# Eight banks and a cap by VectorE in the time-step units, the first dense experts' results copied by ScalarE, and the head's image and text tiles in turns

## What is computed

```python
h = concat([patches @ W_proj.T + b_proj + pos_emb, table[positions(x_txt)]])   # (32, 68, 256)
x = layernorm(h)
u = x @ W_x.T + b_x; g = sigmoid(x @ W_g.T + b_g)                  # 256 -> 512
u = u * g + (conv3(u) + conv_b) * (1 - g)
dt = clip(softplus(x @ W_dt.T + b_dt).mean(axis=(0, 1)), 1e-3, 2)  # mean over all rows
A_d = exp(-softplus(A_raw) * dt); B_d = (A_d - 1) / (A + 1e-6) * B_ssm
y = scan of  state = A_d * state + B_d * u_t,  y_t = sum(state * C_ssm)   # 16 states
h = h + layernorm(x + y @ W_out.T + b_out) * ln_g + ln_b
x = layernorm(h)
top 2 of 4 experts by softmax(layernorm(x) @ router_w.T)
hid = relu(layernorm(x @ w1[e]) * ln_g[e] + ln_b[e])               # 256 -> 512
h = h + layernorm(weighted sum of hid @ w2[e])
```

## Time and profile before

| | us |
|---|---|
| median of 3 runs | 486.98 (486.80 to 487.05) |
| the profiled execution, its own time | 486.0 |
| its span in the trace | 484.2 |
| mean granted clock of PE | 0.979 |

### The profile page before, as it was taken

How to read it: one execution, slowest core, us unless ns; L and a number is a source line. 1 busy time by engine, 2 the same in 40 slices (tenths; PEclk the granted TensorE clock), 3 DMA queues, 4 the chain that set the end, 5 groups by cost and what they waited for, 6 DMA issues and landing times.

```text
span 484.2 us, 10063 instructions
## 1 busy us (share of the span) xinstructions
PE 444.6 (92%) x3208; PEld 375.2 (77%) x3208; DVE 334.0 (69%) x1000; ACT 309.5 (64%) x708; POOL 154.5 (32%) x247
## 2 busy tenths in 40 slices
PE   7988988889899999999998979999999999999982
PEld 5768976767678878878887867878878888888862
DVE  6696645767999334334888968897857548864694
ACT  1773449677965464316666657777787677776882
POOL 5000013484000000002233376377467634526012
PEclk8899999899999999989999989999999999999998
DMA  7944169500029842983511122022222225321421
GB/s 176 198 156 121 48 205 332 175 0 1 1 62 260 201 116 59 219 247 90 196 45 33 67 76 79 11 75 91 84 83 77 78 87 186 104 74 56 142 63 57
DMA packets 54159, 53.62 MB, mean 111 GB/s; under 512 B 24888, under 2 KB 47708, under 8 KB 52828
## 3 DMA queue, kind: packets, MB, share of 16 engines
q1 hardware_dynamic: 50428, 44.46, 34.1%
q0 software_dynamic: 2784, 7.63, 4.2%
q10 hardware_dynamic: 896, 0.89, 0.6%
HBM read 32.40 MB, written 20.58 MB: 109 GB/s over the span
## 4 chain that ended last, share of the span: by engine, by line
PE 48%; DVE 13%; ACT 5%; issue 4%; DMA 4%; SPq 1%; DVEq 0%; ACTq 0%; POOLq 0%
PE bank L1090 12%; PE bank L921 9%; PE bank L461 5%; PE bank L463 4%; PE bank L462 4%; PE bank L997 4%; PE bank L1077 3%; PE bank L941 3%; DVE bsth L1721 1%; PE bank L989 1%; PE bank L1058 1%; ACT U L498 1%; DMA got<-expert_y 1%; DMA xg<-sorted_x 1%; DMA out_dram<-acc 1%
## 5 line engine op out<-in xcount | busy, mean ns | idle before, releaser
L1090 PE MATMUL bank<-w,hr 128*128 (+1 forms) x384 | 92.2, 385 | 7.4 <-DVE ysd L1742 4.3
L1090 PEld LDWEIGHTS bank<-w,hr 128*128 128x128 f32 x384 | 71.1, 191 | 19.0 <-issue 7.8
L678 POOL TENSOR_SCALAR spt<-spt 128x512 f32<-128x512 f32 (+1 forms) x20 | 26.3, 1335 | 80.3 <-ACT spt L1170 80.2
L1294 ACT ACTIVATE hr<-bank,gsel 128x128 f32<-128x128 f32 x128 | 47.9, 460 | 4.7 <-PE bank L1077 4.6
L761 POOL DMA_INDIRECT expert_y<-ysb,toid x32 | 32.7, 1022 | 46.6 <-DVE ysb L1739 37.4
L921 PE MATMUL bank<-Tb,U 68*32 68x68 f32 x1024 | 46.1, 359 | 0.9 <-issue 0.9
L1282 ACT ACTIVATE hn<-bank,nmrh,rsh 128x512 f32<-128x512 f32 x48 | 37.3, 779 | 13.5 <-DVE nmrh L1730 13.4
L1721 DVE BATCH_NORM_STATS2 bsth<-bank 128x6 f32<-128x512 f32 x48 | 33.3, 693 | 15.8 <-PE bank L463 15.3
L921 PEld LDWEIGHTS bank<-Tb,U 68*32 68x32 f32 x1024 | 40.7, 141 | 4.4 <-issue 3.9
L461 PE MATMUL bank<-w_hi,bT_hi 128*128 (+1 forms) x96 | 41.9, 437 | 0.0
L463 PE MATMUL bank<-w_hi,bT_lo 128*128 (+1 forms) x96 | 37.9, 395 | 0.0
(11 more groups left out here) (314 smaller groups left out, 1158.0 us busy)
## 6 DMA issues: line engine op xcount, KB each, us to landing
Tb<-ssm_kernels SPq DMA_DIRECT2D x16, 680.0 KB, 7.4
sorted_x<-zpad SPq DMA_DIRECT2D x5, 1419.0 KB, 14.7
xg<-sorted_x SPq DMA_DIRECT2D x32, 129.0 KB, 2.1
XI<-in_x_dram SPq DMA_DIRECT2D x12, 288.0 KB, 5.5
got<-expert_y SPq DMA_DIRECT2D x13, 256.0 KB, 4.5
h0r<-h_spill SPq DMA_DIRECT2D x17, 128.0 KB, 2.1
out_dram<-acc SPq DMA_DIRECT2D x17, 128.0 KB
w1raw<-in_L_ffn_w_dram SPq DMA_DIRECT2D x4, 512.0 KB, 15.9
```

The source lines that it names most:

```text
L678: pool.tensor_scalar(spt[:, q % 4, 0:w], spt[:, q % 4, 0:w], EXP_CAP, None, ALU.min).then_inc(sem("dt_capped"), 1)
L1090: mm = pe.matmul(bank[second_bank(i)][:, 0:D], hr[:, i % 3, c, :], of_expert(i, w2, c), start=(c == 0), stop=(c == HC - 1))
L1294: last = act.activation(hr[:, i % 3, c, :], bank[turn_bank(i)][:, c * P:(c + 1) * P], ACT.Relu, scale=gain[:, c:c + 1], bias=shift[:, c:c ...
```

## The change

1. The head's tiles stand in turns, text and image; the image pieces come first (12 before the first tile, six in each of the first two steps), without the warm matmuls between them, and `vec` behind them. SP issues the images' DMAs before those of `vec`. The stores of h0 have equal parts of four tiles. The matrix `sel` (128 x 1152, for the bias of image tiles) is made by a select on POOL instead of a copy by DVE.
2. The time-step units use banks by a table, all eight of them in turns, and six buffers `spt`. For units 0 to 7 DVE adds the bias and caps at 40 (`capped`), and ACT makes Exp and Ln in place; units 8 to 19 keep POOL's cap, and ACT's Ln runs two units behind Exp. The convolutions of DVE are cut in two parts (`taps`, `mix`), and the takes stand between them.
3. `w1raw` is loaded by ACT's queue, after the gate of the last block; the halves are made within the scan (`SPLIT_AT`: after v = 26 and 28 on ACT, 27 and 29 on DVE).
4. `ysd` is copied by ACT, ahead of `hr` of the next block.

```diff
-        spt, spj = place(R4, R5, ("spt", [P, 4, 512]), ("spj", [P, 2, 512]))
+        spt, spj = place(R4, R5, ("spt", [P, 6, 512]), ("spj", [P, 2, 512]))
...
-        TILE_ORDER = list(range(NTI, NT)) + list(range(NTI))
-        BLOCK_ORDER = [3, 4, 0, 1, 2]
-
-        H0_OUT = [(0, NH0), (NH0, NH0 + 3), (NH0 + 3, NH0 + 6), (NH0 + 6, NT)]
+        TILE_ORDER = [9, 10, 8, 11, 0, 12, 1, 13, 2, 14, 3, 15, 4, 16, 5, 6, 7]
+        BLOCK_ORDER = [2, 0, 3, 4, 1]
+
+        H0_OUT = [(0, 4), (4, 8), (8, 12), (12, 16), (16, NT)]
...
-        PREP = [("pos", 0), ("pos", 1), ("vec",)] + [("wp", c) for c in range(0, CK, 2)]
+        PREP = [("pos", 0), ("pos", 1)] + [("wp", c) for c in range(0, CK, 2)]
...
-        A_RING = PREP + IMAGES + WEIGHTS
-        LAST_IMAGES = (len(PREP) + len(IMAGES) - 2, len(PREP) + len(IMAGES) - 1)
-
-        A_STEPS = [("ring", q) for q in range(len(PREP))]
-        ahead = list(range(len(PREP), len(A_RING)))
+        A_RING = PREP + IMAGES + [("vec",)] + WEIGHTS
+
+        FIRST_IMAGES = 12
+        A_STEPS = [("ring", q) for q in range(len(PREP) + FIRST_IMAGES)]
+        ahead = list(range(len(PREP) + FIRST_IMAGES, len(A_RING)))
         for k in range(NT + 3):
             A_STEPS += [(f"a{s + 1}", TILE_ORDER[k - s]) for s in (3, 2, 1, 0) if 0 <= k - s < NT]
-            count = 3 if k < NH0 else 1
+            count = 6 if k < 2 else 1 if k < 7 or k >= 15 else 0
...
+            if kind == "b4" and who in ("act", "dve"):
+                return (BLK[i][0] == "early") == (who == "act")
...
+        dt_bank = lambda q: (4, 5, 6, 7, 4, 5, 6, 7, 0, 1, 2, 3, 4, 5, 6, 7, 0, 2, 4, 5)[q]
+        DVE_CAPS = range(2 * HC)
+        POOL_CAPS = [q for q in range(HC * NB) if q not in DVE_CAPS]
...
+        SPLIT_AT = {4 * SV - 6: (0, 1), 4 * SV - 4: (2, 3)}
...
-            act.wait_ge(sem("dt_capped"), q + 1)
-            act.activation(spt[:, q % 4, 0:w], spt[:, q % 4, 0:w], ACT.Ln, bias=onec[:]).then_inc(sem("dt_ln"), 1)
+            if q in DVE_CAPS:
+                act.wait_ge(sem("dt_exp"), q + 1)
+            else:
+                act.wait_ge(sem("exp_capped"), POOL_CAPS.index(q) + 1)
+            act.activation(spt[:, q % 6, 0:w], spt[:, q % 6, 0:w], ACT.Ln, bias=onec[:]).then_inc(sem("dt_ln"), 1)
...
+            sp.dma_start(tabl[:], ins["L0_txt_weights"][0:LT + 2, :]).then_inc(sem("table_in"), 16)
+            for g in range(2):
+                for wp in range(HP):
+                    sp.dma_start(XI[:, g, wp].rearrange("p (y k) -> p y k", k=PWC),
+                                 img[g][:, :, wp * PWC:(wp + 1) * PWC]).then_inc(sem(f"img_in{g}{wp // 3}"), 16)
...
-            for e in range(E):
-                sp.dma_start(w1raw[:, e], ins["L0_ffn_w1"][e].rearrange("(c p) h -> p c h", p=P)).then_inc(
-                    sem("experts_in"), 16)
...
+            pool.wait_ge(sem("rows_zeroed"), 6)
+            pool.affine_select(out=sel[:], in_=sel[:].bitcast(F32), compare_op=ALU.not_equal, fill=1.0, base=0,
+                               pattern=[[-1, LI], [0, B]], channel_multiplier=1).then_inc(sem("rows_zeroed"), 1)
...
-            for q in range(HC * NB):
+            for q in POOL_CAPS:
                 w = BLOCKS[BLOCK_ORDER[q // HC]][1]
                 pool.wait_ge(sem("dt_exp"), q + 1)
-                pool.tensor_scalar(spt[:, q % 4, 0:w], spt[:, q % 4, 0:w], EXP_CAP, None, ALU.min).then_inc(
-                    sem("dt_capped"), 1)
+                pool.tensor_scalar(spt[:, q % 6, 0:w], spt[:, q % 6, 0:w], EXP_CAP, None, ALU.min).then_inc(
+                    sem("exp_capped"), 1)
...
-                if q >= 4:
-                    pe.wait_ge(sem("dt_read"), q - 3)
+                held = [k for k in range(q) if dt_bank(k) == dt_bank(q)]
+                if held:
+                    pe.wait_ge(sem("dt_read"), held[-1] + 1)
+                elif dt_bank(q) < 4:
+                    pe.wait_ge(sem("v_init"), NB)
+                    pe.wait_ge(sem("gate"), NB)
                 elif q >= 2:
...
-                    elif kind == "img":
-                        warm(ps, 1)
...
+                    held = [k for k in range(HC * NB) if dt_bank(k) == first + c % 2]
+                    if c >= NB and held:
+                        pe.wait_ge(sem("dt_read"), held[-1] + 1)
...
-                    act.wait_ge(sem("dt_mm"), q + 1)
-                    act.activation(spt[:, q % 4, 0:w], bank[4 + q % 4][:, 0:w], ACT.Exp,
-                                   bias=vec[:, bdt0 + j:bdt0 + j + 1]).then_inc(sem("dt_exp"), 1)
-                    if q > first:
+                    if q in DVE_CAPS:
+                        act.wait_ge(sem("dt_capped"), DVE_CAPS.index(q) + 1)
+                        act.activation(spt[:, q % 6, 0:w], spt[:, q % 6, 0:w], ACT.Exp).then_inc(sem("dt_exp"), 1)
+                    else:
+                        act.wait_ge(sem("dt_mm"), q + 1)
+                        act.wait_ge(sem("dt_read"), q - 5)
+                        act.activation(spt[:, q % 6, 0:w], bank[dt_bank(q)][:, 0:w], ACT.Exp,
+                                       bias=vec[:, bdt0 + j:bdt0 + j + 1]).then_inc(sem("dt_exp"), 1)
+                    if first < q <= 2 * HC:
                         log1p(act, q - 1)
+                    elif q >= 2 * HC + 2:
+                        log1p(act, q - 2)
+                if end > 2 * HC:
+                    log1p(act, end - 2)
                 log1p(act, end - 1)
...
+                    if (j, nb) == (HC - 1, NB - 1):
+                        for e in range(E):
+                            act.dma_start(w1raw[:, e], ins["L0_ffn_w1"][e].rearrange("(c p) h -> p c h", p=P)).then_inc(
+                                sem("experts_in"), 16)
...
-                    if v == 4 * SV - 4:
-                        for e in range(2):
-                            act.wait_ge(sem("experts_in"), 16 * E)
+                    if v in SPLIT_AT:
+                        act.wait_ge(sem("experts_in"), 16 * E)
+                        for e in SPLIT_AT[v]:
                             copy(w1_hi[:, e], w1raw[:, e]).then_inc(sem("w1_hi"), 1)
...
+                elif kind == "b4":
+                    act.wait_ge(sem("w2_mm"), i + 1)
+                    _, t, e = BLK[i]
+                    copy(ysd[:, t, e, :], bank[second_bank(i)][:, 0:D]).then_inc(sem("yo"), 1)
...
             dve.wait_ge(sem("rows_zeroed"), 6)
-            dve.tensor_copy(sel[0:LI], ident[0:LI, 0:LI].rearrange("p (t o) -> p t o", o=1).broadcast_to([LI, LI, B])
-                            ).then_inc(sem("posb"), 1)
...
+            def capped(q):
+                w, j = BLOCKS[BLOCK_ORDER[q // HC]][1], q % HC
+                dve.wait_ge(sem("dt_mm"), q + 1)
+                dve.tensor_scalar(spt[:, q % 6, 0:w], bank[dt_bank(q)][:, 0:w], vec[:, bdt0 + j:bdt0 + j + 1], 40.0,
+                                  ALU.add, ALU.min).then_inc(sem("dt_capped"), 1)
...
-                taken(q)
-            for nb in range(3):
-                convolve(0, nb)
-            for q in range(AHEAD, 2 * HC - 1):
-                taken(q)
-            convolve(0, 3)
-            for q in range(2 * HC - 1, 2 * HC + 2):
-                taken(q)
+                capped(q)
+                if q >= 2:
+                    taken(q - 2)
+            taken(AHEAD - 2)
+            taken(AHEAD - 1)
+            decay_consts()
+            convolve(0, 0)
+            convolve(0, 1)
+            for q in range(AHEAD, 2 * HC):
+                capped(q)
+            taps(0, 2)
+            taken(4)
+            taken(5)
+            mix(0, 2)
+            taken(6)
+            taken(7)
+            taps(0, 3)
+            taken(8)
+            mix(0, 3)
+            taken(9)
+            taken(10)
             convolve(0, 4)
-            taken(2 * HC + 2)
-            decay_consts()
-            for q in range(2 * HC + 3, HC * NB):
+            for q in range(11, HC * NB):
...
+                    for e in SPLIT_AT.get(v - 1, ()):
+                        dve.wait_ge(sem("w1_hi"), e + 1)
+                        dve.tensor_tensor(w1_lo[:, e], w1raw[:, e], w1_hi[:, e].bitcast(F32), ALU.subtract).then_inc(
+                            sem("w1_split"), 1)
...
-                    elif BLK[i][0] == "early":
-                        _, t, e = BLK[i]
-                        dve.tensor_copy(ysd[:, t, e, :], ps).then_inc(sem("yo"), 1)
```

91 lines of the change are left out of this document (39 added, 52 removed).

## The result

| | before | changed |
|---|---|---|
| median, us | 487.01 (486.80 to 487.98, 4 runs) | 492.21 (489.72 to 493.88, 4 runs) |
| the profiled execution, its own time | 486.0 | 490.81 |
| its span | 484.2 | 488.9 |
| granted clock | 0.979 | 0.978 |

A forecast was written before the change was run, and what follows sets the result against it. PE's own work was taken to bound most of the time, with gains only where PE waits. +2.9 − 3.2 − 0.6 + 0.55 − 3.7 = −4.05 gave 482.9 us for the median; range 474 to 489.5.

The forecast's parts named there:

- The head up to the first image tile: Start of the kernel: first image tile would start at 28.1 us instead of 37.64, 9.5 us earlier.
- The select on POOL: Head: making `sel` on POOL would take 1.3 us, delaying DVE's position chain by nearly all of it, +1.2.
- The turns' chain: Head, text and image steps: PE waits for DVE's 1.91 us up to xs; pairs cost 4.55 or 5.55; +2.9 us.
- The time-step units: Units behind the head: last take would end at 112.3 us instead of 115.54, −3.2 us.
- w1: Scan and its end: loads on ACT's queue stay hidden; −0.6 for a gap, +0.55 for low halves moved into the scan.
- The low half that delays the last copy of y: Scan's end: the last low half (1.2 us) stands ahead of DVE's last copy of y, +0.55 us.
- The gain of 0.6 at the gap of "issue": Scan's end: PE's 0.75 us gap and the slow stretch behind it may go, −0.6 us (0 to −1.4).
- Early dense blocks: Second expert layer: ACT's copy ends PE's waits of 3.17 and 1.13 us for `ysd`; −3.7 us (0 to −5).
- The clock, the rival on the slower side: Head's turns: six gaps of 1.3 to 1.8 us lower PE's clock, 2.4 us per image tile; chance 0.19, 0.18 slower.

The follow-up runs named there:

- the run with xs first: Changed kernel with DVE normalising tile k-2 (xs) before making the low half of tile k-3, against the changed kernel's order: 487.47 us, ratio 1.0009 to the kernel before.

## Why the prediction was wrong

- **The head up to the first image tile: right.** 28.72 against 28.1. The select on POOL, of which no row existed, did no more harm than the 1.3 us put down for it.
- **The turns' chain: right in mechanism, 1.75 us too small.** +4.65 at the waiting unit where the forecast was +2.9, in an execution with full clock. 0.6 of the miss stands at the start (28.72 instead of 28.1), and the pairs cost 4.64 and 5.63 us instead of 4.55 and 5.55, about 0.4 in all; the rest is spread over the last steps. The turns alone with the narrow block second cost 4.5 us by the ratio.
- **The time-step units: right as a sum.** From 46.4 to 43.0 us, −3.3 against the −3.2 forecast. But it is a sum of two things that the prediction did not part: the new units alone take 40.8 (−5.6), and the narrow block's new place gives 2.2 of it back. That the sum came out right is luck. That place was not forced: the changed kernel with the block second ran and had 40.8. And the way through DRAM behind the units, which the sum left at nothing, became 0.8 us longer.
- **w1: −0.05 forecast, +1.5 alone (interval 0 to 3).** The low half that delays the last copy of y was priced well (0.55, and 0.6 in the trace). The gain of 0.6 at the gap of "issue" did not come: the gap was 1.07 us in the changed kernel. The loads, issued at 196.5 instead of 198.5, landed no earlier: ACT still waits for them at 221. What the gap itself waits for is open. The scan of the profiled execution was 1.6 us longer, and the run with the halves alone has the loss (+1.9), the one with the loads alone has none.
- **Early dense blocks: the step that failed, −3.7 forecast and −2.3 alone, nothing of the −3.0 at the place named.** The prediction read "[3.17 <-DVE ysd]" as the cause, and let the product start right behind hr, 3.8 us after the one before. With the copies by ACT alone it started after 5.62 us as before, in the changed kernel after 5.23, and only with the register load moved as well after 3.76. The wait had two ends, DVE's table with the register load behind it, and the copy; the later one has no engine's name. The row of the load, 284.1, was there to be read, and the letter g stood in PE's string just ahead of that block's d.
- **The clock, the rival on the slower side: such gaps do lower it, but it isn't what turned the forecast.** The profiled execution of the changed kernel had clock 1.00 through the whole head and was 4.7 us slower all the same. The rival expected the fall in the turns' gaps. In six of the seven profiled kernels with turns the first image tile ran wholly or partly at half clock, 0.50 to 0.66 from 29 to 34 us, behind a gap of 1.39 to 1.64 us for the images' DMA at 25 us; in the seventh, the changed kernel, that gap was 0.57 us and the clock stayed. A second gap, 1.15 us ahead of the tile, is not what it takes: in the three kernels with the longest first gaps (1.53 to 1.64) the clock was at 0.50 within 0.6 us of the gap's end (windows of half a microsecond), over 2 us ahead of the second one, and in the other three it fell 2.3 to 2.9 us behind the first gap, before the second had ended. PE in the run with xs first, where the 18 transposes take 2.99 us, against 1.18 for 12 in the changed kernel:

```profile
25.38 2.99 PE L830 MATMUL bank<-ident,XI 96*128 96x96 f32 x18 [1.64 <-DMA XI<-in_x_dram]
29.53 0.55 PE L467 MATMUL bank<-WpT_hi,pT_hi 128*128 128x256 f32 x1 [1.15 <-DVE pT_lo L1426]
```

  Of the turns proper, two of the seven show a second stretch of low clock, from 48 to 52 us, behind a gap of 1.90 and 1.91 us; two others with the same gap of 1.91, the changed kernel among them, kept the clock. The first stretch costs 1.5 us and both together 3.5 to 3.7, less than the prediction's 2.4 for each image tile. The Trainium skill's rule on single long gaps (page "TensorE: Matmul & The Clock Gate", section "HAM oscillation — how this bites in real kernels"), weighed in the prediction, has the clock fall behind a long gap; here 1.5 to 1.6 us were enough in three executions, and the measurement decides.
- **The sum, in the profiled execution.** Forecast −4.05, measured +4.7 at the last matmul. The difference of 8.7 us is the turns with the units (1.6), w1 with the scan (1.6), the early blocks (3.6: from the first product of the second layer to the last matmul it is 203.4 us instead of 203.6, which is all that came of the 3.7), and two things that no step had: the way through DRAM behind the units (0.8) and the half clock at 266.6 (1.1). The last isn't the change's own: such a stretch of half clock, with 0.8 to 1.2 us more between the y transposes and the second layer, stands in five of the profiled kernels, three of them without turns. The other runs of the changed kernel add up to 3 us, which half clock in the head, seen in its sister kernels, would explain; their traces were not taken.

## What to carry to other kernels

A gap that is put down to another engine's last signal can have a second end in the waiting engine's own queue: a register load, which no busy time shows, held the next matmul for 1.2 us behind a table here, so look for what stands ahead of the waiting instruction in its own program, then move that as well. When an edit changes the order of pieces of unequal size, price the order: here the narrow piece was cheaper where the pipeline fills than between wide ones. And a row of steps in which PE never waited, like the nine image tiles, is best left together when the steps between which it would be spread end in another engine's chain: turning DVE's order within a step gave 2.4 us back, and the turns still lost.
